# A CIN tower kernel: multiply-and-add field by field on VectorE, first ScalarE bank left in the accumulator

## What is computed

```python
def _cin_layer(X0, Xi, W, b):
    H = W.shape[0]
    F0_, Fi = (X0.shape[1], Xi.shape[1])
    Wr = W.reshape(H, F0_, Fi)
    return jnp.einsum('hjk,bjd,bkd->bhd', Wr, X0, Xi) + b[None, :, None]
X0 = embedded_features            # (512, 39, 16)
Ws = [(W0, b0), (W1, b1), (W2, b2)]
Xi = X0
for W, b in Ws:                   # 128 outputs each
    Xi = _cin_layer(X0, Xi, W, b)
    res.append(Xi.sum(axis=2))
...
h = jnp.concatenate([z, dense_ctx], axis=1)
h = jnp.maximum(h @ W_top1 + b_top1, 0.0)
h = jnp.maximum(h @ W_top2 + b_top2, 0.0)
y = h @ W_top3
```

## Time and profile before

| what | value |
|---|---|
| device time, three runs | 656.97, 657.25, 657.32 us; median 657.25 |
| span of the profiled execution | 664.5 us, 11375 instructions |
| PE busy | 633.7 us, 95% of the span |
| DVE busy | 561.9 us, 85% |
| ACT busy | 557.3 us, 84% |
| POOL busy | 443.1 us, 67% |
| period of one group in the loop | 35.18 us |

### The profile page before, as it was taken

One profiled execution on the slowest core, in us unless ns is written; L12 is line 12 of the kernel. 1 busy time (PEld: TensorE's weight loads), 2 busy tenths in 40 slices (PEclk: granted clock), 3 DMA queues, 4 the chain that ended last, 5 costly groups with the idle time before them and its releaser, 6 DMA issues.

```text
span 664.5 us, 11375 instructions
## 1 busy us (share of the span) xinstructions
PE 633.7 (95%) x2616; PEld 477.0 (72%) x2616; DVE 561.9 (85%) x878; ACT 557.3 (84%) x1940; POOL 443.1 (67%) x504
## 2 busy tenths in 40 slices
PE   2689999999999999999999999999999999989998
PEld 2656767777777777777777777777777777767874
DVE  3538788889899898989898989898989989899890
ACT  2348788989898999999998999998989998999773
POOL 7555897777777778687777787777777535152700
PEclk9799999999999999999999999999999999999999
DMA  8245533242424233242423333323242320200000
GB/s 292 22 61 105 162 38 87 51 87 56 84 56 80 59 58 84 40 102 33 90 41 84 57 86 55 87 52 81 57 85 55 67 68 6 69 27 0 1 0 1
DMA packets 91117, 43.58 MB, mean 66 GB/s; under 512 B 80630, under 2 KB 83780, under 8 KB 88943
## 3 DMA queue, kind: packets, MB, share of 16 engines
q1 hardware_dynamic: 84058, 41.77, 28.1%
q0 software_dynamic: 5120, 1.29, 2.2%
q10 hardware_dynamic: 1904, 0.15, 0.2%
HBM read 36.39 MB, written 1.81 MB: 57 GB/s over the span
## 4 chain that ended last, share of the span: by engine, by line
PE 75%; DVE 8%; ACT 7%; issue 6%; DMA 3%; DVEq 1%; POOL 0%; SPq 0%; another core or an unknown queue 0%
PE yb L1128 16%; PE yb L1124 16%; PE yb L1125 16%; PE p L1089 10%; PE pq L1101 6%; ACT yb L765 5%; DVE x L941 3%; DVE acc L935 3%; DMA gram<-in_L_rec_W_dram 2%; PE yb L1026 2%; DMA emb<-in_table_dram,idx 1%; DVE x1l L896 1%; PE yb L1237 1%; PE p L1182 1%; PE p L1214 1%
## 5 line engine op out<-in xcount | busy, mean ns | idle before, releaser
L765 ACT ACTIVATE yb<-yb,x0t 128x128 f32<-128x128 f32 x1728 | 467.2, 391 | 56.0 <-PE yb L1128 49.6
L935 DVE TENSOR_TENSOR acc<-acc,yb 128x512 f32<-128x512 f32 (+1 forms) x512 | 323.4, 674 | 33.8 <-ACT yb L765 30.9
L1124 PE MATMUL yb<-w1h,x1h 128*128 128x512 f32 (+1 forms) x640 | 293.8, 459 | 5.0 <-DVE acc L935 3.8
L1128 PE MATMUL yb<-w1h,x1l 128*128 128x512 f32 (+1 forms) x640 | 247.4, 387 | 0.0
L1125 PE MATMUL yb<-w1l,x1h 128*128 128x512 f32 (+1 forms) x640 | 247.1, 386 | 0.0
L497 POOL DMA_INDIRECT emb<-in_table_dram,idx x160 | 153.0, 956 | 53.1 <-issue 44.4
L1124 PEld LDWEIGHTS yb<-w1h,x1h 128*128 128x128 f32 x640 | 120.1, 188 | 59.4 <-DVE acc L935 25.3
L1125 PEld LDWEIGHTS yb<-w1l,x1h 128*128 128x128 f32 x640 | 120.5, 188 | 39.6 <-issue 18.0
L1128 PEld LDWEIGHTS yb<-w1h,x1l 128*128 128x128 f32 x640 | 120.1, 188 | 24.8 <-DVE x1l L896 0.4
L568 POOL TENSOR_TENSOR late<-late,x0r 117x512 f32<-117x512 f32 (+1 forms) x105 | 132.7, 1298 | 4.6 <-DMA late<-x_scratch 4.3
L544 POOL TENSOR_TENSOR bdiag<-mask,x0t 128x312 f32<-128x312 f32 x64 | 45.7, 714 | 107.0 <-PE pq L1101 106.4
(11 more groups left out here) (124 smaller groups left out, 377.2 us busy)
## 6 DMA issues: line engine op xcount, KB each, us to landing
late<-x_scratch SPq DMA_DIRECT2D x45, 312.0 KB
late<-x_scratch SPq DMA_DIRECT2D x30, 234.0 KB
x0r<-x_scratch SPq DMA_DIRECT2D x15, 234.0 KB
emb<-in_table_dram,idx POOLq DMA_INDIRECT x160
gram<-in_L_rec_W_dram SPq DMA_DIRECT2D x1, 2496.0 KB
late<-x_scratch SPq DMA_DIRECT2D x15, 156.0 KB
spare<-spare SPq DMA_DIRECT2D x28, 78.0 KB
x_scratch<-emb SPq DMA_DIRECT2D x75, 20.0 KB
```

The lines of the kernel that those rows point to most:

```text
L765: op = act.activation(part, part, ACT.Copy, scale=x0t[u][:, t, j:j + 1])
L935: dve.tensor_tensor(part, part, parts(y_bank(t, m), n), ALU.add).then_inc(summed, 1)
L1124: pe.matmul(y[:, 0:w], hi, w1h[:, at:at + w], start=True, stop=False)
L1128: pe.matmul(y[:, 0:w], lo, w1h[:, at:at + w], start=False, stop=True).then_inc(bank_ready, 1)
```

## The change

DVE's three banks are no longer scaled as wholes. Each of their 12 fields is one instruction of 128x128 (`fuse`): field times column plus partial sum, written to one of two partial sums by turns; the first adds the bias `b1c` in place of a partial sum, the second only multiplies. Every field from the third on waits until the field two before it is written. ACT writes its first bank (bank 1) into parts 0 to 3 of the accumulator, and DVE adds only the other six ACT banks, all into those four parts, each waiting for the addition before it. The accumulator has 6 parts in place of 9 and is laid out part by part, so the additions run over consecutive values, while the fold reads values 128 apart. The fold now stands behind bank 9's addition in every tile; `SEAM_ORDER` is gone. PE may reuse bank 1 when ACT has scaled it, and bank 6 when its last field is in. DVE's loop over groups is written out.

```diff
-N_ACC = 2
-BEGINS = DVE_BANKS[0:N_ACC]
-PARTS = N_ACC * BANK_F + 1
-DVE_ORDER = (("sum before", 8), ("scale", 0), ("sum before", 9), ("scale", 3), ("sum", 1), ("sum", 2),
-             ("sum", 4), ("fold before", 0), ("scale", 6), ("sum", 5), ("sum", 7), ("sum", 6))
-SEAM_ORDER = tuple(x for x in DVE_ORDER if x[0] != "fold before") + (("fold before", 0),)
-SUM_ORDER = (1, 2, 4, 5, 7, 6, 8, 9)
+FIRST_BANK = ACT_BANKS[0]
+FUSED_AT = BANK_F
+N_FUSED_PARTS = 2
+PARTS = BANK_F + N_FUSED_PARTS
+DVE_ORDER = (("sum before", 8), ("fuse", 0), ("sum before", 9), ("fold before", 0), ("fuse", 3), ("sum", 2),
+             ("sum", 4), ("fuse", 6), ("sum", 5), ("sum", 7))
+SUM_ORDER = (2, 4, 5, 7, 8, 9)
...
-        acc = [sb(f"acc{u}", [P, HID, PARTS]) for u in range(2)]
+        acc = [sb(f"acc{u}", [P, PARTS, HID]) for u in range(2)]
...
+                if m == FIRST_BANK and at_least(T, 2):
+                    act.wait_ge(x2_ready, T - 1)
...
-                    op = act.activation(part, part, ACT.Copy, scale=x0t[u][:, t, j:j + 1])
+                    dst = acc[t % 2][:, i, :] if m == FIRST_BANK else part
+                    op = act.activation(dst, part, ACT.Copy, scale=x0t[u][:, t, j:j + 1])
...
-            act.wait_ge(b1_in, 16)
-            for u in range(2):
-                act.activation(acc[u][:, :, PARTS - 1], b1c[:, :], ACT.Copy).then_inc(bias_ready, 1)
...
+                for i in range(fields_of(m)):
+                    j = BANK_F * m + i
+                    k = fused_before(m) + i
+                    part = acc[t % 2][:, FUSED_AT + k % N_FUSED_PARTS, :]
+                    field, x = y[:, i * HID:(i + 1) * HID], x0t[u][:, t, j:j + 1]
+                    if k == 0:
+                        dve.scalar_tensor_tensor(out=part, in0=field, scalar=x, in1=b1c[:, :],
+                                                 op0=ALU.mult, op1=ALU.add).then_inc(fused, 1)
+                    elif k < N_FUSED_PARTS:
+                        dve.tensor_scalar(part, field, x, None, ALU.mult).then_inc(fused, 1)
+                    else:
+                        dve.wait_ge(fused, T * N_FUSED + k - N_FUSED_PARTS + 1)
+                        dve.scalar_tensor_tensor(out=part, in0=field, scalar=x, in1=part,
+                                                 op0=ALU.mult, op1=ALU.add).then_inc(fused, 1)
...
-                dve.tensor_reduce(x2[t % 2][:, :], acc[t % 2][:, :, :], AX.X, ALU.add).then_inc(x2_ready, 1)
+                dve.tensor_reduce(x2[t % 2][:, :], acc[t % 2][:, :, :].rearrange("p j h -> p h j"), AX.X,
+                                  ALU.add).then_inc(x2_ready, 1)
...
-            with dve.Fori(1, GROUPS // 2 - 1) as it:
+            for it in range(1, GROUPS // 2 - 1):
...
-                if m in BEGINS:
-                    pe.wait_ge(dve_scaled, T * N_DVE + BEGINS.index(m) + 1)
+                if m in DVE_BANKS:
+                    pe.wait_ge(fused, T * N_FUSED + fused_before(m) + fields_of(m))
+                elif m == FIRST_BANK:
+                    pe.wait_ge(act_scaled, T * N_ACT + 1)
                 else:
                     pe.wait_ge(summed, sums_by(T, m))
```

More of the change, by code:

```diff
@@ L257, in tower @@
         act_scaled = sem("act_scaled")
-        dve_scaled = sem("dve_scaled")
+        fused = sem("fused")
         summed = sem("summed")
@@ L299, in sums_by, with fused_before @@
             return T * N_SUM + SUM_ORDER.index(m) + 1
+        N_FUSED = sum(fields_of(m) for m in DVE_BANKS)
+        def fused_before(m):
+            return sum(fields_of(k) for k in DVE_BANKS if k < m)
         ACT_SPLIT = tuple(c for c in SPLIT if c in ACT_HIGH)
@@ L439, in period @@
                         sp.sem_inc(sp_waited, 1)
-                        sp.wait_ge(dve_scaled, g * (TILES * N_DVE))
+                        sp.wait_ge(fused, g * (TILES * N_FUSED))
                         sp.sem_inc(sp_waited, 1)
@@ L898, in low_part, with fuse @@
                                          op1=ALU.subtract).then_inc(x1l_ready, 1)
-            def parts(y, n):
-                return y[:, 0:n * HID].rearrange("p (j h) -> p h j", h=HID)
-            def scale(g, t, u, m):
+            def fuse(g, t, u, m):
                 T = g * TILES + t
@@ L908, in scale @@
                 dve.wait_ge(bank_ready, T * BANKS + m + 1)
+                if m == DVE_BANKS[0] and at_least(T, 2):
+                    dve.wait_ge(x2_ready, T - 1)
                 y = y_bank(t, m)
-                if m in BEGINS:
[L911 to L915, removed]
-                                      ALU.mult).then_inc(dve_scaled, 1)
-                    return
@@ L922, in add_bank @@
             def add_bank(T, t, m):
                 n = fields_of(m)
-                k = SUM_ORDER.index(m)
-                if k < N_ACC:
-                    dve.wait_ge(dve_scaled, T * N_DVE + k + 1)
-                else:
-                    dve.wait_ge(summed, sums_by(T, m) - N_ACC)
-                if m in ACT_BANKS:
-                    dve.wait_ge(act_scaled, T * N_ACT + ACT_BANKS.index(m) + 1)
-                else:
-                    dve.wait_ge(dve_scaled, T * N_DVE + DVE_BANKS.index(m) + 1)
@@ L933, in add_bank @@
-                at = BANK_F * (k % N_ACC)
-                part = acc[t % 2][:, :, at:at + n]
-                dve.tensor_tensor(part, part, parts(y_bank(t, m), n), ALU.add).then_inc(summed, 1)
+                if m != SUM_ORDER[0]:
+                    dve.wait_ge(summed, sums_by(T, m) - 1)
+                dve.wait_ge(act_scaled, T * N_ACT + ACT_BANKS.index(m) + 1)
+                part = acc[t % 2][:, 0:n, :]
+                dve.tensor_tensor(part, part, y_bank(t, m)[:, 0:n * HID].rearrange("p (j h) -> p j h", h=HID),
+                                  ALU.add).then_inc(summed, 1)
@@ L937, in fold @@
             def fold(T, t):
                 dve.wait_ge(summed, (T + 1) * N_SUM)
+                dve.wait_ge(fused, (T + 1) * N_FUSED)
                 if at_least(T, 2):
                     dve.wait_ge(gram_done, T - 1)
-                dve.tensor_reduce(x2[t % 2][:, :], acc[t % 2][:, :, :], AX.X, ALU.add).then_inc(x2_ready, 1)
+                dve.tensor_reduce(x2[t % 2][:, :], acc[t % 2][:, :, :].rearrange("p j h -> p h j"), AX.X,
+                                  ALU.add).then_inc(x2_ready, 1)
@@ L945, in period @@
                     T = g * TILES + t
-                    for kind, m in SEAM_ORDER if t == TILES - 1 and more else DVE_ORDER:
-                        if kind == "scale":
-                            scale(g, t, u, m)
+                    for kind, m in DVE_ORDER:
+                        if kind == "fuse":
+                            fuse(g, t, u, m)
                         elif kind == "sum":
```

7 lines of the change are left out of this document (2 added, 5 removed).

## The result

The changed kernel takes **659.91 us** (median of 6 runs, 658.68 to 661.12) beside 657.29 us for the kernel before (6 runs on the same chip). The ratio is 1.0039, 95% interval 1.0029 to 1.005: slower by 2.6 us, small but clear of the 0.2% that can be told from no change. The forecast was 658.7, slower, with DVE's dearer work eating what the seam gives.

What follows compares the result with a forecast made beforehand. PE was taken as busiest (95%), standing still at group seams, with DVE setting the last group's pace. Seams +0.8, first two groups +0.3 and last group +0.4 make +1.5 on 657.25: 658.7 us, range 649 to 670.

Steps and rivals of the forecast that it cites:

- Field: One 128x128 multiply-add on DVE: 0.26 us, taken from the row of `x1l`; twelve a tile are 3.12 us.
- Neighbour waits: Four times a tile a DVE instruction waits for its direct neighbour: 0.12 us each, 0.48 together.
- Fold: DVE's fold of 768 values read singly 512 bytes apart: 1.5 us, or 0.86 if the distance costs nothing.
- The walk of the seam: Between groups: bank 5's addition 0.5 us later, waits at gram product (0.35) and bank 4 (0.09) gone; net +0.06.
- The baseline: The kernel before, from its first profile: a group takes 35.18 us, and PE loses 0.67 us at each seam.
- The first two groups and the last: First two: bank 2's addition later behind the fold, +0.3 us; last: DVE's pace counts, +0.4 at the last fold.
- Written-out DVE code removes register instructions that ran beside other work: DVE's loop over groups written out: no effect on the time, no term in the sum.
- Rival 1: DVE becomes the bound once a field exceeds 0.265 us or the fold 1.56: slower, 669 us; chance 0.25.
- Rival 2: Fields at 0.22 us and fold at 0.86 to 1.2 on DVE: faster, 651 us; chance 0.22.
- Rival 3: At the seam the wait for bank 5 moves to another releaser, nothing changes: 657 us; chance 0.08.

Runs made afterwards that it cites:

- before, second profile: The kernel before, profiled again with no edit: 657.1 us, span 655.3 us, a group 35.10 us.

## Why the prediction was right, and where not

The time (658.7 for 659.9) and its sign held, by the mechanism of the forecast. Its size did not quite: +1.5 us was forecast, +2.6 measured. The spans of the profiled executions, cut by the second matmul of bank 0 in groups 2 and 15 and by the end of the last fold (us):

| | before, second profile | changed | before, fold moved alone | changed, fold's reads in sequence |
|---|---|---|---|---|
| groups 0 and 1 | 73.96 | 74.88 | 74.04 | 73.43 |
| groups 2 to 14 | 456.37 | 457.71 | 449.37 | 450.69 |
| group 15 to the last fold's end | 38.66 | 39.47 | 37.62 | 36.41 |
| ahead of and behind these | 86.3 | 86.1 | 86.2 | 87.4 |
| span | 655.3 | 658.2 | 647.2 | 647.9 |

Step by step:

- *Field*: 0.26 us forecast, 0.26 found. The scalar column's price did not overlap, and a wait for the field two before is free.
- *Neighbour waits*: 0.12 forecast, 0.11 found. *Fold*: 1.5 forecast, 1.43 to 1.45 found; the estimate by the Trainium skill's page "Vector Engine (DVE) Microarchitecture Reference", section 5.2, 1.4, was as near. A tile is 12 x 0.26 + 5 x 0.60 + 0.46 + 4 x 0.11 + 1.43 = 8.4 us and a group 34.4 (forecast 8.57 and 34.9). The trace agrees: DVE stands still once a group, for 0.72 us, and works 34.5.
- *The walk of the seam*: about 0.7 us ahead of bank 1 and nothing at the gram product or bank 4 was forecast; 0.70 and nothing was found. Bank 3 was to start 0.09 us late, without the working in full: its first field starts 290.94 - 287.22 = 3.72 us ahead of bank 0's second matmul, where the scaling stood 298.34 - 294.53 = 3.81 ahead. Group 35.2 to 35.3 forecast, 35.23 found; DVE busy near 36 of 37, found 35.73.
- *The baseline*: the first profile gave 35.18 us a group for before, the second 35.10. Against the latter a seam costs 0.13 us, not 0.06, and groups 2 to 14 cost 1.3 us, not 0.8. That is 0.70 lost at bank 1 less 0.57 won behind it, where 0.50 and 0.44 were forecast from the first profile. Both terms were too small, and that so little is left of them is in part luck.
- *The first two groups and the last*: +0.3 and +0.4 were forecast, +0.9 and +0.8 found. The last group's is a term that was too small. The first two groups' can't be put down to the change: with the loop put back (whose code is the same there) they take 73.75 us, less than before.
- *"Written-out DVE code removes register instructions that ran beside other work"*: the step that failed. It was put at nothing. In the kernel before the same edit costs 1.3 us, of which 0.7 by waits that became instructions of their own. That the same 1.3 us stands inside the changed kernel's 2.6 is not shown; it has only 14 late waits for ACT from 100 to 580 us, where the second profile of before has 55, and going back costs it 20 us. That a term of nothing did no harm to the sum is luck: the loop could not have been kept at its old price.

**Rival 1** (DVE the bound) did not come: 0.26 stayed under the forecast's own threshold of 0.265, and the fold under 1.56. The run with one partial sum shows what it looks like, at 703 us, not the "over 730" of the text, which made every field wait. **Rival 2** (cheap side) was right in its fold alone: with a fold of 0.87 and fields still at 0.26 the time is 649.9, where it said 651 with cheaper fields as well. **Rival 3** (nothing changes) is out for the change: the wait at bank 1 grew as forecast, and the fold's place moved the time in both kernels. But a wait that only moves to another releaser is just what the earlier addition of bank 5 showed, 659.4 for 659.9 us.

What the forecast did not do was to ask, of its net of +0.06 us a seam, whether gain and loss belong together. They are 0.6 and 0.7 us, and the gain is to be had alone: the kernel before with its fold ahead of bank 3 is the fastest of all measured, 649.1 us.

## What to carry to other kernels

A change that nets out near zero is best taken apart on paper first: list what moves work into a hole of the late engine and what makes that engine's work dearer, and run the first without the second. When an engine is late over a whole stretch, reordering its work within the stretch moves the wait from one consumer to the next; only less work in the stretch, or work moved into a hole ahead of it, takes it away. Ask of each layout which instructions hop in single values in SBUF. The old one had none among its scalings, additions and folds; with fields one by one, in the two layouts that were run, either the fold hops, once a tile, or the fields and the additions do, 18 times.

## What the runs showed of the hardware

- A wait that has to be an instruction of its own, since the instruction behind it carries another, started the addition 102 ns after the end of what it waited for, in place of 32 (the kernel before, with its loop and written out).
- A direct wait for the instruction ahead on DVE costs 0.11 us at 128x512 and 0.13 at 128x128; one for the instruction two before costs nothing (0.26 us from field to field with it and without).
- Hops at every value in SBUF cost about 0.86 ns a value on DVE's additions, where one source and the result hop ((1124 - 683) / 512), 0.74 on its fold, where the source does ((1524 - 953) / 768), and 1.0 on ACT's writes ((511 - 382) / 128).
- A hop of 512 bytes at every value in PSUM cost DVE's additions nothing (687 ns with it, 683 without), nor did hops between runs of four in SBUF.
- A loop whose body had grown from 270 to 376 rows of the trace kept DVE's sequencer from its next instruction for 2.8 us at each turn, with three instruction packets behind each branch; the shorter one of before went on after 0.2, with none.
